# A two-layer transformer block on one core: the order of its first DMAs, and the place where layer 1's weights are folded

## What is computed

```python
x = x + _L0_attn_ref(_layernorm(x), ...)   # 16 heads, phi(q) (phi(k)^T v), linear attention
x = x + _L0_ffn_ref(_layernorm(x), ...)    # silu(x w1) * (x w2); gelu(. h1); gelu(. h2); . w3
x = x + _L1_attn_ref(_layernorm(x), ...)   # one head of 256, softmax
x = x + _L1_ffn_ref(_layernorm(x), ...)    # tanh(x weight aux1 aux2 + bias)
```

## Time and profile before

| what | value |
|---|---|
| median of 3 runs | 2127.78 us (2126.31 to 2128.02) |
| profiled execution, its own time: span from first to last instruction | 2125.2 us |
| TensorE matmuls busy (PE) | 2016.7 us, 95% |
| VectorE (DVE) / ScalarE (ACT) / GpSimd (POOL) busy | 57% / 39% / 18% |
| mean granted TensorE clock | 0.985 |
| data moved by DMA | 48.68 MB |

### The profile page before, as it was taken

One profiled execution on the slowest core, in us unless ns is written; L12 is line 12 of the kernel. 1 busy time (PEld: TensorE's weight loads), 2 busy tenths in 40 slices (PEclk: granted clock), 3 DMA queues, 4 the chain that ended last, 5 costly groups with the idle time before them and its releaser, 6 DMA issues.

```text
span 2125.2 us, 40501 instructions
## 1 busy us (share of the span) xinstructions
PE 2016.7 (95%) x15484; PEld 1938.4 (91%) x15484; DVE 1208.1 (57%) x2880; ACT 837.6 (39%) x1538; POOL 373.5 (18%) x347
## 2 busy tenths in 40 slices
PE   6899999999999999999999999999999999999985
PEld 5899999999999999999999999998999999999985
DVE  5556656465565645656365565655656466565544
ACT  2334434344443444434344343444434344343422
POOL 1111212012121011211012121121211112121011
PEclk9999999999999999999999999999999999999997
DMA  9400000000000000000000000000000000000000
GB/s 364 181 3 3 23 3 16 9 2 22 2 23 3 2 22 3 22 3 12 12 2 22 3 22 3 2 23 2 22 3 2 23 2 12 3 12 2 2 13 10
DMA packets 24567, 48.68 MB, mean 23 GB/s; under 512 B 1152, under 2 KB 21376, under 8 KB 24064
## 3 DMA queue, kind: packets, MB, share of 16 engines
q1 hardware_dynamic: 24240, 43.41, 5.8%
HBM read 35.02 MB, written 19.92 MB: 26 GB/s over the span
## 4 chain that ended last, share of the span: by engine, by line
PE 80%; DVE 6%; POOL 4%; issue 4%; ACT 3%; DMA 3%; SPq 0%; DVEq 0%; POOLq 0%; ACTq 0%
PE ffn_fill L834 43%; PE att_fill L798 23%; PE ffn_fill L892 6%; PE ffn_fill L798 5%; POOL act_lo L488 3%; PE att_fill L850 2%; DVE whole L570 2%; PE att_fill L968 1%; DMA scratch_h2T<-in_h2T 1%; DMA scratch_h1T<-in_h1T 1%; POOL rstd_C L475 1%; ACT L728 1%; ACT xt_hi L719 1%; DVE st L505 1%; DVE act_hi L575 1%
## 5 line engine op out<-in xcount | busy, mean ns | idle before, releaser
L834 PE MATMUL ffn_fill<-act_hi,h 128*128 128x256 f32 x4096 | 989.6, 284 | 9.2 <-POOL act_lo L488 3.5
L834 PE MATMUL ffn_fill<-act_lo,h 128*128 128x256 f32 x4096 | 980.6, 281 | 0.0
L834 PEld LDWEIGHTS ffn_fill<-act_hi,h 128*128 128x128 f32 x4096 | 773.5, 189 | 16.6 <-POOL act_lo L488 6.9
L834 PEld LDWEIGHTS ffn_fill<-act_lo,h 128*128 128x128 f32 x4096 | 774.6, 189 | 3.7
L579 DVE CAST act_hi<-whole 128x512 fp32r<-128x512 f32 x256 | 110.0, 430 | 572.0 <-ACT whole L737 572.0
L737 ACT ACTIVATE whole<-ffn_fill,scales 128x256 f32<-128x256 f32 x512 | 215.1, 472 | 556.5 <-PE ffn_fill L834 555.6
L798 PE MATMUL ffn_fill<-half_hi,w 128*128 128x256 f32 x1024 | 264.4, 297 | 40.6 <-issue 30.6
L798 PE MATMUL ffn_fill<-half_lo,w 128*128 128x256 f32 x1024 | 257.7, 290 | 0.0
L798 PEld LDWEIGHTS ffn_fill<-half_hi,w 128*128 128x128 f32 x1024 | 202.7, 198 | 47.6 <-issue 46.4
L488 POOL TENSOR_TENSOR act_lo<-whole,act_hi 128x512 fp32r<-128x512 f32 x128 | 166.6, 1301 | 410.9 <-DVE act_hi L575 410.3
L475 POOL TENSOR_TENSOR rstd_B<-var_eps_B,minus_half 128x2 f32<-128x2 f32 x32 | 22.6, 707 | 1131.5 <-DVE var_eps_B L512 1131.5
(11 more groups left out here) (155 smaller groups left out, 3155.0 us busy)
## 6 DMA issues: line engine op xcount, KB each, us to landing
x<-in_L_attn_x SPq DMA_DIRECT2D x16, 512.0 KB, 4.0
out<-x SPq DMA_DIRECT2D x16, 512.0 KB, 3.0
h<-scratch_h1T SPq DMA_DIRECT2D x1, 4096.0 KB, 16.2
h<-scratch_h2T SPq DMA_DIRECT2D x1, 4096.0 KB, 14.0
w<-scratch_w1T SPq DMA_DIRECT2D x1, 1024.0 KB, 14.6
w<-scratch_w2T SPq DMA_DIRECT2D x1, 1024.0 KB, 17.3
w<-scratch_w3T SPq DMA_DIRECT2D x1, 1024.0 KB, 5.8
rows<-in_rows SPq DMA_DIRECT2D x1, 640.0 KB, 6.3
```

Source lines behind the costliest of these rows:

```text
L834: last = pe.matmul(two(bank)[:, o, :], view(w), view(moving[:, k, :]), start=k == 0 and o == 0 and half == 0, stop=k == KH - 1 and half == ...
```

## The change

SP's order of the first DMAs is another. Before: seven raw L1 matrices, copies of layers 0 and 1, landings of 0 and 1, copy of 2, landing of 2, copy of 3, landing of 3. Now: copies of layers 0 and 1, six raw matrices, landing of 0, copy of 2, the seventh raw matrix (behind waits for layer 0's attention of tile 0, since it now lies in `xn`), landing of 1, copy of 3, landings of 2 and 3.

The steps FOLD0, TAKE0, FOLD1, TAKE1 and WIDE leave `PROLOGUE`: WIDE now stands behind CHECK1, FOLD0 and TAKE0 behind G0, FOLD1 and TAKE1 behind G1. LOOK00 stands ahead of AO, LOOK01 ahead of BNO0. The four looks at `h1`, of which two stood ahead of U0 and two behind U1 and U2, now stand one behind each of U0 to U3. The first look at `h2` stands behind G1 and no longer behind G0. `raw_a2` and `t1` lie in `xn`, `bv_wide` in `kv_b`, `bk_wide` in a buffer of its own. SP's wait for FOLD1 is counted through `FIRST`.

```diff
--- before.py
+++ after.py
@@ -197,11 +197,12 @@
 
 
 PROLOGUE = steps_from("""
-    a:AST a:ANO a:AB PREP a:T a:AKV0 SCALE a:AKV1 a:AKV2 a:AKV3 a:AS a:AQ a:AM a:AO FOLD0 WIDE
-    n:BST0 n:BNO0 TAKE0 n:BT0 FOLD1 LOOK00 TAKE1 LOOK01 CHECK0 LOOK10 LOOK11""")
+    a:AST a:ANO a:AB PREP a:T a:AKV0 SCALE a:AKV1 a:AKV2 a:AKV3 a:AS a:AQ a:AM LOOK00 a:AO
+    n:BST0 LOOK01 n:BNO0 n:BT0 CHECK0""")
 FIRST = with_checks(only("", "a", "n"), {
-    ("U", 1): "LOOK12", ("U", 2): "LOOK13", ("U", 3): "CHECK1", ("G", 0): "LOOK20", ("G", 1): "LOOK21 LOOK22",
-    ("G", 2): "LOOK23", ("G", 3): "CHECK2 LOOK30", ("H", 0): "CHECK3"})
+    ("U", 0): "LOOK10", ("U", 1): "LOOK11", ("U", 2): "LOOK12", ("U", 3): "LOOK13 CHECK1 WIDE",
+    ("G", 0): "FOLD0 TAKE0", ("G", 1): "FOLD1 TAKE1 LOOK20", ("G", 2): "LOOK21 LOOK22",
+    ("G", 3): "LOOK23 CHECK2 LOOK30", ("H", 0): "CHECK3"})
 BODY = PLAN
 LAST = only("", "c")
 TAIL = only("c")
@@ -287,11 +288,9 @@
         raw_wq = gated[:, 0]
         raw = [x[:, 1 + n // 2, 2 * (n % 2):2 * (n % 2) + 2, :] for n in range(6)]
         raw_q, raw_k, raw_v, raw_out, raw_f, raw_a1 = raw
-        spare = whole[:].rearrange("p a b n -> p (a b n)")
-        raw_a2 = spare[:, 0:512].rearrange("p (k n) -> p k n", k=KD)
-        t1 = gated[:, 1]
-        bk_wide = spare[:, 512:768].rearrange("p (k n) -> p k n", k=KD)
-        bv_wide = spare[:, 768:1024].rearrange("p (k n) -> p k n", k=KD)
+        raw_a2, t1 = xn[:, 0:2, :], xn[:, 2:4, :]
+        bk_wide = sb("bk_wide", [P, KD, P])
+        bv_wide = kv_b[:, 3, :].rearrange("p (k n) -> p k n", k=KD)
         squares = kv_b[:].rearrange("p a d -> p (a d)")
 
         full = {r: [sem(f"{r}_full{b}") for b in range(RING)] for r in banks}
@@ -410,21 +409,27 @@
                     sp.dma_start(tile.bitcast(F32), a["scratch_" + name].rearrange("(k p) n -> p k n", p=P))\
                       .then_inc(w_loaded[layer], 16)
 
-            for tile, name in ((raw_q, "L1_attn_w_q"), (raw_k, "L1_attn_w_k"), (raw_v, "L1_attn_w_v"),
-                               (raw_out, "woutT"), (raw_f, "wfT"), (raw_a1, "L1_ffn_aux_weight1"),
-                               (raw_a2, "L1_ffn_aux_weight2")):
-                sp.dma_start(tile, km(name)).then_inc(c_loaded, 16)
+            after_as = Counts(phases[0])
+            for step in PROLOGUE[:PROLOGUE.index(("AS", 0, "a"))]:
+                after_as.ahead(step)
             bounce(0)
             bounce(1)
+            for tile, name in ((raw_q, "L1_attn_w_q"), (raw_k, "L1_attn_w_k"), (raw_v, "L1_attn_w_v"),
+                               (raw_out, "woutT"), (raw_f, "wfT"), (raw_a1, "L1_ffn_aux_weight1")):
+                sp.dma_start(tile, km(name)).then_inc(c_loaded, 16)
             land(0)
+            bounce(2)
+            sp.wait_ge(s["phik_ready"], NB)
+            sp.wait_ge(s["phiq_ready"], 2)
+            wait_taken(sp, after_as, "att_fill", 0)
+            sp.dma_start(raw_a2, km("L1_ffn_aux_weight2")).then_inc(c_loaded, 16)
             land(1)
-            bounce(2)
+            bounce(3)
             land(2)
-            bounce(3)
             land(3)
 
             c = Counts(phases[0])
-            for step in PROLOGUE:
+            for step in PROLOGUE + FIRST:
                 if step[:2] == ("FOLD", 1):
                     wait_taken(sp, c, "att_fill", 2)
                 c.ahead(step)
```

## The result

| | before | changed |
|---|---|---|
| median of 4 runs each | 2127.05 us (2126.00 to 2128.02) | 2149.29 us (2144.55 to 2152.35) |
| profiled execution: span | 2125.2 us | 2149.3 us (its time: 2151.03) |
| H0 of tile 0 starts | 84.85 us | 106.64 us |
| mean granted TensorE clock | 0.985 | 0.979 |

The changed kernel is slower: the ratio is 1.0099, with a 95% interval of 1.0087 to 1.0111. Forecast were 2148.3 us and slower.

What follows compares the result with a forecast made beforehand. TensorE is busy 95% of the span, so the start of tile 0's H0 sets the end. H0 at 105.3, 20.5 us late: 2125.2 + 20.5 = 2145.7 span, plus 2.6 gives 2148.3 us; range 2139 to 2154.

Steps and rivals of the forecast that it cites:

- U0: Tile 0's first U step: at about 47, 8.2 us after `w1`, `w2` land; not what counts, as `h1` lands later.
- G0: Tile 0's first G step: starts at 73.1 against 61.83 before, and takes 5.57 us at the low clock.
- The queue as a line: First DMAs: transfers end in issue order, so `h1` lands at 61.7, 11.9 us later, behind `h2`'s copy.
- The folding without its cover: G steps of tile 0: the folding's 10.3 us, free before under the DMAs, now cost their length.
- rival A: DMA queue: `h1`'s landing gets past `h2`'s copy; G0 at 63.9, H0 at 96.1, 2139.1 us; chance 0.07.
- Behind H0: After H0 of tile 0: nothing waits, so the 20.5 us by which H0 is late carry to the end.
- B: DMA queue: copies and landings run side by side; H0 at 87.1, 2130.0 us, no change; chance 0.05.
- C: G steps: a 1.71 us TensorE pause for no releaser returns; 2150.0 us; inside the forecast's range, 0.86 together with it.

Runs made afterwards that it cites:

- e1: The changed kernel with the copy of `h2` put back behind the landing of `h1`, folding still in the G steps: 2138.67 us, ratio 1.0058.
- e2: The kernel before with only the new order of the first DMAs, all seven raw matrices behind the first copies, folding and looks unmoved: 2136.48 us, ratio 1.0040.
- e4: The changed kernel with the folding and its takes moved behind U0, into the wait for `h1`: 2140.69 us, ratio 1.0060.
- e3: The changed kernel with 6 of the folding's 26 matmuls left, each one column wide: 2190.64 us, ratio 1.0298.
- e5: The changed kernel with every folding matmul kept but one column wide: 2143.62 us, ratio 1.0067.
- e12: The kernel before with `h2` copied and landed in halves, earlier looks and CHECK2, and 20 one-column filler matmuls at TensorE's program start: 2122.65 us, ratio 0.9980.
- e9: The kernel before with 44 one-column fp32 filler matmuls at the start of TensorE's program: 2181.54 us, ratio 1.0250.
- e10: The kernel before with 20 one-column fp32 filler matmuls at the start of TensorE's program: 2127.07 us, ratio 0.9991.

## Why the prediction held

Step by step, forecast against the profiled execution of the changed kernel:

| step | forecast | measured |
|---|---|---|
| `w1`, `w2` landed | 38.9 | 39.5 |
| copy of `h2` ended | 49.9 | 50.9 |
| `h1` landed | 61.7 | 62.2 |
| `h2` landed | about 75 | 75.6 |
| U0 | about 47 | 49.0 |
| G0 starts | 73.1 | 73.62 |
| G0 takes | 5.57 | 6.71 |
| FOLD0, FOLD1 | 5.34, 4.96 | 5.18, 4.79 |
| G3 ends | 100.3 | about 101.7 |
| H0 starts | 105.3 | 106.64 |

**The queue as a line** held, with its prices: the four ends in the table are within 1.0 us. It isn't a strict line, since the first raw matrix ended 1.4 us ahead of the copy issued before it, but nothing waited on that. e1 and e2 show it from both sides: `h1` landed at 49.5 with the copy behind it, at 62.2 with the copy ahead, on otherwise different kernels.

**The folding without its cover** held: 10.3 us forecast, 9.97 on the chain, and e4 gives 8.35 back at H0 by moving it to where the engines stand.

**U0** came 2 us later than forecast, and it cost nothing, as argued: behind it everything waited for `h1`. That the looks moved behind U0 would cost something without this wait is what e1 shows, 2.75 us; the prediction had 2.8 for it in rival A.

**What was mis-sized**: G0. I took 5.57 us for it from H0 before, whose low clock lasts for a part of it. In the changed kernel the clock stayed at 0.50 up to 78 and G0 took 6.71. With that 1.1 and the 0.5 of `h1`, less 0.3 in the folding, H0 is 1.3 late on the forecast. The other way, I took 2.6 us between the span and a run's time; the profiled execution has 1.7. That part was the medians' scatter.

**Behind H0** the offset to before should stay at 21.8. At the first store it is 21.8 (259.92 - 238.09), at later ones 21.2 to 23.9 without a trend, at the end 24.1 (2149.3 - 2125.2). The medians differ by 22.2. For the other 2.3 us in the profiled execution I found no place; that they are scatter of the loop's passes is likely and not shown.

**Luck** is in how near the medians came, 1.0 us. The span of the profiled execution was 3.6 us above the forecast (2149.3 against 2145.7), 1.3 of it at H0 and 2.3 behind it. Against that stand the 0.9 between 2.6 and 1.7, and the 1.7 by which the median of the four runs lies below the profiled one. The mechanism holds by H0, not by the median.

**Rival A** (`h1` gets past the copy) and **B** (side by side) fell with `h1` at 62.2. **C** (a pause in the G steps) didn't come: TensorE's chain from 73.62 to 97.88 has no "issue" in it. I had put C aside because the DMA traffic would be over, and that reason was wrong. e2 has pauses of 1.31 and 1.25 us ahead of G1 and G2, the first with the queue empty. Its program for TensorE is that of the kernel before, which pauses at the same two steps. The changed program has no pause in its G steps in any of its five runs with a trace (the changed kernel, e1, e3, e4, e5), whatever the traffic. So C most likely stayed away because TensorE's program is laid out otherwise, and it was luck that the forecast left it out.

**Not foreseen**, and without cost here: SP stood 12.68 us on the issue of one 256 KB matrix and 3.93 on the next, so that the landings of `w1` and `w2` were issued at 26.47 and 27.30, not at about 17 when their copies ended. In a line that is busy with `h1`'s copy until 30.1 (6.29 + 23.8) that is no loss.

Open is why e5 gained so much in the median and so little at H0, and where the last microsecond of e12's median comes from. Whether ACT and its own queue for some of these DMAs would let `h1` past a copy wasn't tried.

## What to carry to other kernels

Large transfers on one queue were a line here: order them by when they are needed, and a copy that only serves a later stage belongs behind the landing that the next stage waits for, even if that leaves copies side by side. Work that was hidden in a wait cost its full length once it stood where its engine was the bound, so ask of a move what covered it before and what does after. And whoever times a kernel with a few instructions taken out or put in ahead of a loop must look at the loop's period first: it moved by some 3% here for a reason that has nothing to do with the work removed.

## What the runs showed of the hardware

- **The loop's place in TensorE's program.** A pass begins with a pause of 2.0 to 2.7 us. At the placements of e3 (80 instructions fewer) and e9 (176 more) there are two such pauses, and a pass takes 131.8 and 131.4 us, not 128.0; over 14 passes that is some 50 us. At the placements of before and e10 (80 more) there is one such pause; e10 has some more of 0.2 to 0.6 us, and its passes still take 127.8 us. Other shifts weren't tried. The page's first part doesn't show this: the share of "issue" in TensorE's waits does, and the packets of kind "instruction" go with it in part (317, but 330 or 331 in e3, e9 and e10).
- **Pauses in single steps move with the program too.** Ahead of G1 and G2 they are 0.60 and 1.71 us in the kernel before and 1.31 and 1.25 in e2, where the queue was empty during the first. In e10 one of 1.20 us stands ahead of G3, and the runs of the changed program have none in the G steps.
- **The order of ends on one queue isn't strict.** A 256 KB matrix issued 1.1 us behind a 4 MB copy landed at 28.7, 1.4 us ahead of that copy's end. The 4 MB transfers all ended in the order of issue.
- **An issue can block.** With three copies and four raw matrices issued ahead of it (2 + 4 + 1 MB), SP stood 12.68 us on one issue, and 11.59 to 12.81 us on the same one in e1 to e5. Behind a blocked issue stand all later ones, whatever they need.
- **A one-column fp32 matmul isn't free, nor of one price.** In e9 the 88 records of the filler took 18.93 us, 0.215 each; in e5 the 52 records of the folding took 6.44 us, 0.124 each. The rows give a granted clock of 1.00 in both stretches (6 to 8 us, 80 to 84 us). But that column can't be trusted so early: in the kernel before it reads 1.00 at 14 to 16 us and at 18 to 20 us, though matmuls of 512 columns start 0.43 us apart at 15 us and 0.23 at 19. Behind the filler of e9 they are 0.43 apart too. So the filler most likely ran at the lower level. Taking nearly all columns from the folding's products saved a third of their time (9.97 to 6.44 us), and the granted clock in the step behind them fell to 0.50.
